# Neighbour sums of a graph convolution placed between the message groups of the last node tile

## The reference, cut to what matters

```
agg  = segment_sum(x[src], edge_type * n + dst)         # per relation and target node
mean = agg / max(cnt, 1)
h1   = einsum('rni,rio->no', mean, W_rel) + x @ W_root + b_rgcn
xw   = h1 @ W_gcn
norm = dinv[src] * dinv[dst]
out  = segment_sum(xw[src] * norm, dst) + xw * dinv**2 + b_gcn
```

## Time and profile before

| | us |
|---|---|
| median of 3 runs | 1624.33 |
| lowest and highest of them | 1621.21, 1628.65 |
| the profiled execution, whole | 1621.66 |
| its span, first to last instruction | 1619.9 |
| messages on PE (lines 2345 and 2360), first start to the last one's end | 1193.2 to 1327.2 |
| neighbour sums on PE (line 2379) | 1327.46 to 1360.18 |
| matmuls with `W_gcn` on PE (line 2398), first start | 1361.13 |

### The profile page before, as it was taken

How to read it: one execution, slowest core, us unless ns; L and a number is a source line. 1 busy time by engine, 2 the same in 40 slices (tenths; PEclk the granted TensorE clock), 3 DMA queues, 4 the chain that set the end, 5 groups by cost and what they waited for, 6 DMA issues and landing times.

```text
span 1619.9 us, 23123 instructions
## 1 busy us (share of the span) xinstructions
PE 1439.9 (89%) x7904; PEld 1149.5 (71%) x7904; DVE 932.9 (58%) x2154; ACT 533.5 (33%) x601; POOL 579.6 (36%) x500
## 2 busy tenths in 40 slices
PE   8998957769689999399999999999978989989992
PEld 7887647755355555299999999999955765556661
DVE  6643658862744563366555566655547961466664
ACT  0001025631211101245555555555425641113330
POOL 0000077777676566332221222222137740111102
PEclk9999977879789999599999999999989999999996
DMA  7102900001104412477777877777759871326635
GB/s 192 35 0 4 122 2 2 2 1 27 34 3 111 163 37 65 112 253 271 274 280 281 289 272 268 275 272 284 263 190 327 275 229 54 98 88 190 206 121 165
DMA packets 114255, 248.50 MB, mean 153 GB/s; under 512 B 30461, under 2 KB 52154, under 8 KB 114092
## 3 DMA queue, kind: packets, MB, share of 16 engines
q1 hardware_dynamic: 79228, 141.18, 28.4%
q0 software_dynamic: 22432, 72.27, 15.9%
q10 hardware_dynamic: 12528, 34.22, 5.3%
HBM read 206.77 MB, written 45.31 MB: 156 GB/s over the span
## 4 chain that ended last, share of the span: by engine, by line
PE 52%; POOL 18%; DMA 11%; issue 10%; DVE 4%; ACT 2%; SPq 1%; POOLq 1%; ACTq 0%; DVEq 0%; PEldq 0%
PE PS L2250 24%; PE PS L2002 8%; POOL evwb L664 6%; POOL zidxb L666 5%; PE PS L2431 4%; POOL edge_dram L683 4%; PE PS L2442 3%; PE PS L2240 3%; PE PS L2398 2%; DMA edge_dram<-recb,idxb 2%; PE PS L2379 2%; DMA zidxb<-zrow_dram,idxb 2%; DMA xg<-xn_dram,xrow 2%; DMA pre<-z_dram,grow 2%; DVE mlo L1770 2%
## 5 line engine op out<-in xcount | busy, mean ns | idle before, releaser
L693 POOL DMA_INDIRECT xg<-xn_dram,xrow x70 | 118.0, 1686 | 374.2 <-DVEq L1305 363.2
L2250 PE MATMUL PS<-whi,xhi 128*128 128x384 f32 x840 | 222.1, 345 | 2.3 <-DVEq L1622 2.3
L2250 PE MATMUL PS<-whi,xlo 128*128 128x384 f32 x840 | 215.3, 337 | 0.0
L2250 PE MATMUL PS<-wlo,xhi 128*128 128x384 f32 x840 | 213.9, 336 | 0.0
L1127 DVE TENSOR_TENSOR wlo<-raw,whi 128x2304 fp32r<-128x2304 f32 x72 | 184.5, 2563 | 38.6 <-ACTq L918 31.4
L1127 DVE TENSOR_TENSOR xlo<-PS,xhi 128x768 fp32r<-128x768 f32 x70 | 67.1, 958 | 162.0 <-ACTq L927 157.1
L916 ACT ACTIVATE whi<-raw 128x2304 fp32r<-128x2304 f32 x72 | 153.6, 2134 | 12.5 <-ACT xhi L926 5.8
L2250 PEld LDWEIGHTS PS<-wlo,xhi 128*128 128x128 f32 x840 | 152.9, 189 | 0.0
L2250 PEld LDWEIGHTS PS<-whi,xlo 128*128 128x128 f32 x840 | 152.3, 189 | 0.0
L2250 PEld LDWEIGHTS PS<-whi,xhi 128*128 128x128 f32 x840 | 148.9, 189 | 2.6 <-DVEq L1622 2.6
L2002 PE MATMUL PS<-hot_dr,hot_s 125*125 125x512 bf16 (+9 forms) x880 | 133.8, 300 | 5.9 <-DVE hot_dr L1184 5.9
(11 more groups left out here) (368 smaller groups left out, 2428.6 us busy)
## 6 DMA issues: line engine op xcount, KB each, us to landing
raw<-in_L_gnn_W_rel SPq DMA_DIRECT2D x72, 1152.0 KB, 7.8
z_dram<-xn ACTq DMA_DIRECT2D x70, 384.0 KB, 5.6
wroot<-in_L_ffn_w SPq DMA_DIRECT2D x12, 576.0 KB, 5.1
y_dram<-yb ACTq DMA_DIRECT2D x17, 384.0 KB, 3.7
pre<-in_L_ffn_w SPq DMA_DIRECT2D x9, 576.0 KB, 5.3
gw<-in_L_gnn_W SPq DMA_DIRECT2D x2, 2304.0 KB, 27.3
fw<-in_L_ffn_w SPq DMA_DIRECT2D x8, 576.0 KB, 6.0
fw<-in_L_ffn_w SPq DMA_DIRECT2D x1, 4608.0 KB, 20.6
```

Source lines behind the costliest of these rows:

```text
L693: pool.indirect_dma_start(xg[b][j][:, :], None, xn_dram, bass.IndirectOffsetOnAxis(ap=xrow[:, b, j:j + 1], axis=0)).then_inc(x_gathered[b] ...
L2250: mm = pe.matmul(slot(q)[:, s * BANK:s * BANK + HALF], a[:, k, :], wt[:, k, s * HALF:(s + 1) * HALF], start=(k == 0 and part == 0), stop=( ...
```

## The change

Twelve of the thirty neighbour sums, those of blocks 0, 1 and 2 over node tiles 0 to 3, are issued between the message groups of the last tile. `SUMS_AT` maps the group's number within the tile to the block and node tile whose sum stands behind it: behind groups 0, 1, 3 the sums of block 0 over tiles 0, 1, 2; behind 4, 6, 7 those of block 1; behind 11 and 12 the sums of blocks 0 and 1 over tile 3; behind 13 to 16 those of block 2 over tiles 0 to 3. Each waits for `h1_ready` of its tile. `gcn_sum` itself is the same and only stands further up. The branch for crowded inputs (`largest > GE`), whose lines do not show in this profile, gets the twelve sums at its end.

```diff
+SUMS_AT = dict(zip((0, 1, 3, 4, 6, 7, 11, 12, 13, 14, 15, 16),
+                   [(k, t) for k in range(2) for t in range(T - 2)] + [(k, T - 2) for k in range(2)] + [(2, t) for t in range(T - 1)]))
...
                             if piece == 0:
                                 take("messages", later % 4, later // 4)
                             root_piece(later, *ROOT_PIECES[piece])
+                        if n == T - 1 and piece in SUMS_AT:
+                            k, tile = SUMS_AT[piece]
+                            pe.wait_ge(h1_ready, tile + 1)
+                            gcn_sum(k, [tile])
                     pe.wait_ge(msg_used, (n + 1) * GT)
                     pe.sem_inc(full[n % 4], 1)
...
-            pe.wait_ge(h1_ready, T - 1)
-            for k in range(3):
-                gcn_sum(k, range(T - 1))
             pe.wait_ge(h1_ready, T)
             for k in range(3):
                 gcn_sum(k, [T - 1])
```

More of the change, by code:

```diff
@@ L2318, in scatter, with gcn_sum @@
                 mm.then_inc(msg_used, 1)
+            def gcn_sum(k, tiles):
+                q, n = GCN_SUM[k]
+                if 0 in tiles:
+                    take("gcn_sum", q, n)
+                for t in tiles:
+                    for o, m in ((0, BANK), (BANK, N - BANK)):
+                        mm = pe.matmul(slot(q)[:, o:o + m], h1[:, t, k * 128:(k + 1) * 128], cnt[:, t, o:o + m],
+                                       start=(t == 0), stop=(t == T - 1), skip_group_check=True)
+                if T - 1 in tiles:
+                    mm.then_inc(full[q], 1)
             largest = pe.value_load(crowded[0:1, 0:1], min_val=0, max_val=EDGES)
@@ L2341, in _ @@
                 pe.sem_inc(full[0], 1)
+                pe.wait_ge(h1_ready, T)
+                for k in range(3):
+                    gcn_sum(k, range(T - 1))
             with pe.Else():
```

## The result

The changed kernel took 1622.08 us, median of 18 runs (1608.32 to 1628.44); the kernel before, run beside it, 1629.49 (18 runs, 1621.21 to 1637.05). The ratio is 0.9946, 95% interval 0.9926 to 0.9966: 0.54% less time, or 5.5 to 12.1 us of 1629.49. The two medians are 7.4 us apart, the ratio alone says 8.8; both lie within that interval. The forecast was 0.55% less (9.0 of 1621.66), and its absolute time, 1615.3 with a range to 1619.5, missed.

What follows compares the result with a forecast made beforehand. In the last tile PE waits for gathered rows, then neighbour sums alone bound it. 13.0 us of sums leave, 4.04 return, seams and tile's end 0: 9.0 gained, 1612.7 profiled, 1615.3 as median; range 1611.3 to 1619.5.

Steps and rivals of the forecast that it cites:

- Slack: Last message tile: 8.96 us of PE slack hides moved sums; distance (first group to first `W_gcn` matmul) 46.0, not 55.1.
- Seams: 23 new changes between sum and group in the last tile: taken as 0 us, at most 4.4 for all.
- second rival: Each change between sum and group costs a 0.19 us weight load: 4.4 in all, gain 4.6, time 1619.7; chance 0.05.
- Groups late to PE: Last tile: buffers released later still refill in time; tightest at groups 8 to 11, with 0.3 us to spare.
- The tile's end: After the last group: one sum covers tile 4's copy, PE pauses 0.4 us as before, so 0 added.
- first rival: Tile 4's copy stands in the open, as PE's sequencer doesn't run ahead: gain 7.9 us, time 1616.4; chance 0.09.
- Clock: Last tile: a fall to half clock now costs about 1.65 us, so the gain is 7.4 to 10.7 us.
- fourth rival: PE at half clock from the last tile on, through 25 us of work: 16 us worse, time 1640; chance 0.04.
- Behind the sums: After the neighbour sums: everything follows as before, so the whole 9.0 us gain is passed on.
- Last gather: Last tile: PE's delay doesn't reach the last gather's issue; 8 us lie between, so nothing moves.
- the base of the time: Whole kernel: the three-run median of 1624.33 us, 2.67 above the profiled execution, from which 1615.3 was forecast.
- rival 3: Other executions have more slack in the last tile, hiding up to all 13.0 us: time 1611.3; chance 0.10.

Runs made afterwards that it cites:

- nocover: Changed kernel with block 2's sum over tile 3 moved from behind the last group to ahead of it: 1628.40 us, ratio 0.9958 to the kernel before; distance grows by 1.08.
- both: Changed kernel, five moved sums earlier in tiles 2 and 3, two behind the last group, `W_gcn` started with five of six blocks evicted: 1621.92 us, ratio 0.9950.
- the repetition: The changed kernel, unchanged, timed and profiled once more: 1624.92 us, ratio 0.9924 to the kernel before.
- deep6: Changed kernel with the ring of `mhi`, `mlo` and `hotf` six deep instead of four: 1630.34 us, ratio 0.9956 to the kernel before.
- six: Only the six sums of blocks 0 and 1 over tiles 0 to 2 moved, against the kernel before: 1628.39 us, ratio 0.9967.
- twice: Changed kernel with each of the twelve moved sums issued twice in a row: 1637.63 us, ratio 1.0035 to the kernel before.

## Why the prediction was right, and where it was wrong

**The mechanism held in most steps.**

- *Slack*: 8.96 us forecast, distance 46.0 forecast and 46.26 found, against the one profile of before that the forecast was read from.
- *Seams*: none costs a weight load; 1.785 us for a pair is 0.70 + 1.083, which is the 0 that I took, against the second rival's 0.19 each.
- *Groups late to PE*: no wait for `mlo` is marked in tile 4 of the first two profiles of the changed kernel; in the third there are two above 0.15 (0.17 and 1.36). The 1.36 stands before group 11, where I had found "0.3 us to spare": in that profile late gathers held up the groups before it (ACT waited 1.05 us for the one at 1320.50), and the copy of tile 3 came on top. Group 11 started 16.64 us behind the tile's first there, and 14.38 in the first profile; that is 2.26 us, all by which 48.52 exceeds 46.26. My own sign of being wrong, "if groups wait for `mlo` behind group 10", is thus met in one profile of three.
- *The tile's end*: the pause is 0.38, forecast 0.4, and the copy starts at 1340.13, 1.07 behind the last group's start, beside the sum. That the sequencer runs past the branch, and the first rival is wrong, is shown by nocover's 1.08.
- *Clock*: 1.00 throughout tile 4 in all three profiles, so not the fourth rival. That a fall there costs about 1.65 us is borne out by the 1.6 of both.
- *Behind the sums*: 19.75 and 0.95 as before, and nothing comes back: from the first `W_gcn` matmul to the end 256.7 us, against 258.8, and over all profiles of either kernel it is 254.8 to 259.8.
- *Last gather*: issued 10.3 us behind the tile's first group, where it was 12.25, and over all profiles 9.1 to 16.8 against 9.6 to 18.5 in the kernel before, so nothing shows that PE's delay reaches it.

The ratio, 0.9946, is the forecast's 0.9944. That it agrees so closely is luck: its interval is 0.9926 to 0.9966, and the repetition gave 0.9924.

**The step that failed is the base of the time**: "That one is 2.67 below the median of the runs, 1624.33; with the same distance, 1615.3 us". The gain was taken off a median of three. Over 18 runs that same kernel's median is 1629.49, 5.2 us higher. The measured ratio on the old base gives 0.9946 x 1624.33 = 1615.6, the forecast; the forecast ratio on the new one gives 1629.49 x 0.9944 = 1620.4, with 1622.08 measured. So of the 6.8 us by which 1615.3 was missed, 5.2 are the base. With it fails the range, "from rival 3 (1611.3) to just short of rival 2, 1619.5": it is made of mechanisms alone. The same two gains, 13.0 and 4.6, taken off 1629.49 give 1616.5 to 1624.9, which holds 1622.08. Single runs of before spread over 15.8 us, those of the changed kernel over 20.1. In the later experiments the medians of the same kernel before were 1633.14, 1637.2 and 1630.6, so its time also moves by several us from one set of runs to the next. I had quoted the 7.4 us spread of the three runs for the chances and not for the range.

**One reading was mostly wrong.** "So in this tile PE waits for gathered rows" leaves out DVE. A group costs DVE 0.19 + 0.93 us from start to start, 1.12 in all, where PE needs 0.70, and the tile has a copy of 0.95 on top. The idle 1.36 us before 1319.21 was the copy of tile 3, which DVE did at 1316.74, ahead of that group's `mlo`. It stands there as 1.37 in the three other profiles of before. The window of tile 4 in the fourth profile of before, where the episode had let the gathers get ahead (columns as in the earlier trace rows):

```profile
1317.00:1335.00 18.00, 15.07 (x61) 11.41 (x62) 17.75 (x32) 13.12 (x15) 9.99 (x6) 0.91 0.54 163
```

DVE is busy 17.75 of 18.00 us. There the distance is 53.62, and 53.62 - 46.26 = 7.4 us of slack are DVE's pace alone; late gathers add up to 60.54 - 53.62 = 6.9 more: in the second profile ACT waits for a gather before each of the 16 `mhi` from 1312.10 to 1335.88, 0.22 to 0.98 us. By this measure, an estimate, 7.36 of the 8.81 us won against the first profile were DVE's pace and 55.07 - 53.62 = 1.45 late gathers. The size of the slack was right; what made it was for the greater part something else. The third rival, more slack in other executions, is thus part of the truth: over four and three profiles the mean distances are 57.04 and 47.01, 10.0 us apart. That lies within the 7.4 to 10.7 given, with the profiles of before 6.9 us apart among themselves.

**Why the two first profiles differ by only 1.2 us.** Tile 3 held an episode in the one and none in the other, 32.94 against 23.62 us. It explains this pair of profiles, not the timing over many runs. Whether episodes are more frequent in the changed kernels stays open: eight of ten of changed kernels have one (deep6's by the rows above), two of four of before. That is too few to tell.

## What to carry to other kernels

Independent matmuls placed where PE waits for its operands are free up to the slack, which is read from the engine that feeds PE as well as from the transfers; past it they cost their full price (six and twice). A sum behind the last group covers the copy that the next stage waits for, at no cost of its own. Forecast a ratio from the mechanism, and put an absolute time around it only with the scatter of the base included: a median of three runs was 5.2 us off where the effect was 9.

## What the hardware showed that I had not expected

In some stretches PE's semaphore raises take effect late. In episodes of some 10 to 20 us, `hotf` starts up to 14 us after the matmuls that release its buffer have ended, each time later than for the group before; in the worst profile, six's, DVE stood idle for 18.9 us in all this way. The trace also keeps the times at which a semaphore changed. In the changed kernel's first profile `msg_used` changed for groups 54 to 57 at 1291.50, 1295.04, 1299.26 and 1303.48, where their matmuls are given as ended at 1287.79, 1289.14, 1290.49 and 1291.84, and each `hotf` started 0.02 to 0.03 us behind the change. In the same stretch of the kernel before's first profile each change stands 0.01 to 0.02 us behind the matmuls' end. So it is not the waiting engine that is late, but the change of the semaphore. In six four changes come together, at 1226.08, 1226.15, 1226.23 and 1226.31. The profile's ends of matmuls are modelled, so a late raise can't be told here from matmuls that ended late. The granted clock was 0.50 (1.2 GHz) in most of such a stretch in the changed kernel, 1298.5 to 1308.7, where PE was busy 6.39 of 10.20 us. Two groups more of buffering don't cover it. Transfers went on at 259 GB/s there, not far from the 269 of the half-clock stretch in the earlier trace rows, so moved bytes alone don't mark an episode. The cause wasn't found.
